# Two cross attentions of a perceiver-style block: one projection run per step in the first, a re-ordered hand-over before the main loop of the second

## The reference

```
# first cross attention (32 heads of 16)
q = layernorm(x) @ Wq.T ;  k_raw = ctx @ Wk.T ;  v_raw = ctx @ Wv.T      # k and v interleaved per head
scores = rmsnorm(q) . rmsnorm(k) * 16**-0.5
x = x + softmax(scores) @ v
...
# second cross attention (16 heads of 32)
qdq(t): s = max(|t|) / 127 over the last axis ;  round(t / s) * s
q = qdq(layernorm(x)) @ qdq(wq).T + bq ;  k, v = split(ctx @ wkv.T + bkv)
o = softmax(q . k / sqrt(32)) @ v
x = x + qdq(o) @ qdq(wp).T + bp
```

## Time and profile before

| | |
|---|---|
| median of three runs | 1500.7 us (1500.62 to 1502.13) |
| the profiled execution's own time | 1501.55 us |
| its span, first to last instruction | 1499.7 us |
| PE busy | 1398.5 us, 93% of the span |
| DVE busy | 1009.4 us, 67% |
| ACT busy | 784.4 us, 52% |
| POOL busy | 82.0 us, 5% |
| first cross attention, main loop | about 36 to 437 us |
| second cross attention, c2 | about 773 to 1012 us |
| c3, c4, c5 | about 1012 to 1020, 1020 to 1174 and 1174 to 1194 us |

### The profile page before, as it was taken

The page is one execution under the profiler, slowest core; times in us unless marked ns, Lnnn a source line. Parts: engine busy times, 40 slices in busy tenths (PEclk is TensorE's granted clock), DMA queues, the critical chain, the costliest instruction groups (busy, mean ns, idle before and its releaser), DMA issues. The chain is left out here.

```text
span 1499.7 us, 31832 instructions
## 1 busy us (share of the span) xinstructions
PE 1398.5 (93%) x11742; PEld 1075.1 (72%) x11742; DVE 1009.4 (67%) x1657; ACT 784.4 (52%) x1134; POOL 82.0 (5%) x73
## 2 busy tenths in 40 slices
PE   6999999999979989999989999978999598899998
PEld 4677776777745468999978787755666365899997
DVE  7666667666654557666647777876999843676664
ACT  3677777777750635554432232227888203555553
POOL 0000000000000400000001111111000000000000
PEclk8999999999999989999999999988999769899999
DMA  5333453333324058565305223218777120676662
GB/s 159 73 84 85 114 115 80 85 86 86 65 64 161 1 203 270 188 213 194 100 29 176 105 107 131 84 57 184 172 172 164 42 55 6 215 255 209 215 219 78
DMA packets 133599, 191.20 MB, mean 127 GB/s; under 512 B 74987, under 2 KB 96717, under 8 KB 130317
## 3 DMA queue, kind: packets, MB, share of 16 engines
q1 hardware_dynamic: 133533, 190.30, 43.7%
HBM read 154.12 MB, written 17.48 MB: 114 GB/s over the span
## 5 line engine op out<-in xcount | busy, mean ns | idle before, releaser
L187 PE MATMUL psum<-m_x_hi,m_gu_hi 128*128 128x256 f32 x780 | 222.2, 285 | 1.8 <-DVE m_h L2406 1.5
L188 PE MATMUL psum<-m_x_hi,m_gu_lo 128*128 128x256 f32 x780 | 221.7, 284 | 0.0
L189 PE MATMUL psum<-m_x_lo,m_gu_hi 128*128 128x256 f32 x780 | 221.6, 284 | 0.0
L1543 DVE TENSOR_REDUCE x_peaks<-psum 128x2048 f32 (+1 forms) x64 | 146.3, 2291 | 50.6 <-PE psum L1421 50.6
L187 PE MATMUL psum<-x_w_hi,x_ctx_hi 128*128 128x256 f32 x512 | 158.6, 310 | 0.0
L187 PEld LDWEIGHTS psum<-m_x_hi,m_gu_hi 128*128 128x128 f32 x780 | 150.1, 192 | 5.4 <-DVE m_h L2406 2.0
L188 PEld LDWEIGHTS psum<-m_x_hi,m_gu_lo 128*128 128x128 f32 x780 | 150.1, 192 | 1.5
L189 PEld LDWEIGHTS psum<-m_x_lo,m_gu_hi 128*128 128x128 f32 x780 | 150.1, 192 | 0.0
L1700 DVE TENSOR_TENSOR e_wqp<-e_wqp,x_probs 128x1024 f32<-128x1024 f32 x124 | 143.1, 1227 | 2.7 <-ACT x_probs L1715 2.5
L188 PE MATMUL psum<-x_w_hi,x_ctx_lo 128*128 128x256 f32 x512 | 144.5, 282 | 0.0
L189 PE MATMUL psum<-x_w_lo,x_ctx_hi 128*128 128x256 f32 x512 | 144.3, 282 | 0.0
(11 more groups left out here) (319 smaller groups left out, 2765.7 us busy)
## 6 DMA issues: line engine op xcount, KB each, us to landing
m_gu_raw<-in_m_gu SPq DMA_DIRECT2D x41, 768.0 KB, 4.2
e_w<-x_keys_dram SPq DMA_DIRECT2D x45, 512.0 KB, 6.8
m_gu_raw<-in_m_gu SPq DMA_DIRECT2D x18, 1024.0 KB, 4.9
x_ctx_raw<-in_ctxT SPq DMA_DIRECT2D x64, 256.0 KB, 2.7
m_dn_raw<-in_m_down SPq DMA_DIRECT2D x16, 768.0 KB, 4.3
m_dn_raw<-in_m_down SPq DMA_DIRECT2D x18, 512.0 KB, 5.1
x_keys_dram<-x_keys_hi SPq DMA_DIRECT2D x16, 512.0 KB, 3.2
x_keys_dram<-e_wqp SPq DMA_DIRECT2D x16, 512.0 KB, 2.7
```

What stands on the lines that cost most here:

```text
L187: pe.matmul(out, a[0], b[0], start=start, stop=False, skip_group_check=True)
L188: pe.matmul(out, a[1], b[0], start=False, stop=False, skip_group_check=True)
L189: return pe.matmul(out, a[0], b[1], start=False, stop=stop, skip_group_check=True)
L1543: dve.tensor_reduce(peaks[:, t, 4 * m:4 * m + 4, bass.ds(k, 1)].rearrange("p h k -> p (h k)"), g.psum[:, at:at + BANKS, :], AX, ALU.max).t ...
```

## The change

Four things are done.

1. In the first cross attention, PE does all of `values` for step n+1 (12 matmuls) in one run behind `keys`, and nothing behind `weigh`. Since the value bank is now full before `weigh` of step n-1 has read the old values, ACT waits for `pv_done` before `take_values`.
2. In c3, PE turns the peaks first and zeroes the banks behind it. The spread of the `wp` scales goes from c3 to c5, where ACT, PE and ACT again do it at the block's start, with waits on `wp_row_taken`. ACT's first Exp with its table load goes from the start of c4 to the end of ACT's list in c3.
3. The loads of `bp` and `bv` go from the start of c4 into c2, behind the twelve DMAs of `q_stack`. The bias add goes from POOL in c4 to DVE in c3. The load of key pair 1 goes from c3 to the start of c4.
4. Names and semaphores follow.

```diff
@@ first cross attention, PE
-                        values((s + 1) % SLOTS, half_of(at + 1), v_part, range(NC // 2))
+                        values((s + 1) % SLOTS, half_of(at + 1), v_part, range(NC))
                     for grp in (2, 3):
                         score(n, s, half, grp)
...
                     for grp in (0, 1):
                         weigh(n, s, grp)
-                    if at + 1 < STEPS:
-                        values((s + 1) % SLOTS, half_of(at + 1), v_part, range(NC // 2, NC))
@@ first cross attention, ACT
                     if at + 1 < STEPS:
+                        act.wait_ge(pv_done, 4 * n + HG)
                         take_values(n + 1, s + 1, v_part)
@@ second, c2, SP (behind the q_stack DMAs)
+                    sp.dma_start(bp[:, :], A["x1_bp"]).then_inc(bp_loaded, 16)
+                    sp.dma_start(bv[:, :], A["x1_bv"]).then_inc(bv_loaded, 16)
@@ second, c3
                     dve.tensor_scalar(peakT[:, :], g.bank[0][0:Y_H, 0:L], -1.0, None, ALU.mult).then_inc(peak_taken, 1)
+                    dve.wait_ge(bp_loaded, 16)
+                    for t in range(NT):
+                        dve.tensor_tensor(g.x[:, t, :], g.x[:, t, :], bp[:, :], ALU.add)
...
-                    for b in g.bank[4:8]:
-                        pe.matmul(b[:, :], g.zeros[:, 0:P], g.zeros[:, :], start=True, stop=False, ...)
                     pe.wait_ge(peak_found, 1)
                     for t in range(NT):
                         last = pe.transpose(g.bank[0][0:Y_H, t * P:(t + 1) * P], peak[:, t, :], g.ident[:, :])
                     last.then_inc(peak_turned, 1)
-                    pe.wait_ge(wp_spread_ready, NC)
-                    for m in range(NC):
-                        last = pe.transpose(g.bank[1][:, m * P:(m + 1) * P], wp_spread[:, m, :], g.ident[:, :])
-                    last.then_inc(wp_row_turned, 1)
+                    for b in g.bank[4:8]:
+                        pe.matmul(b[:, :], g.zeros[:, 0:P], g.zeros[:, :], start=True, stop=False, ...)
...
-                    (four spreads into wp_spread, the wait, the copy to wp_row)
                     act.activation(k_stack[3 * Y_HD:3 * Y_HD + 1, 1, :, :]...)
+                    act.activation(warm[:, :], g.zeros[:, 0:1], ACT.Exp)
...
                     load_keys(sp, 0, 0, slice(NC // 2, NC))
-                    load_keys(sp, 1, 1)
                     sp.wait_ge(peak_placed, 16)
@@ second, c4
-                    pool.wait_ge(bp_loaded, 16)
-                    for t in range(NT):
-                        pool.tensor_tensor(g.x[:, t, :], g.x[:, t, :], bp[:, :], ALU.add)
...
-                    sp.dma_start(bp[:, :], A["x1_bp"]).then_inc(bp_loaded, 16)
-                    sp.dma_start(bv[:, :], A["x1_bv"]).then_inc(bv_loaded, 16)
+                    load_keys(sp, 1, 1)
...
-                    act.activation(warm[:, :], g.zeros[:, 0:1], ACT.Exp)
@@ second, c5: the spread of the wp scales, now into a part of vals and bank 2
+                    for m in range(NC):
+                        act.activation(wp_spread[:, m, :], g.zeros[:, 0:P], ACT.Identity,
+                                       bias=g.x1_grid[:, 1, m:m + 1]).then_inc(wp_spread_ready, 1)
+                    act.wait_ge(wp_row_turned, 1)
+                    act.activation(wp_row[:, :], g.bank[2][:, :], ACT.Copy).then_inc(wp_row_taken, 1)
...
+                    pe.wait_ge(wp_spread_ready, NC)
+                    for m in range(NC):
+                        last = pe.transpose(g.bank[2][:, m * P:(m + 1) * P], wp_spread[:, m, :], g.ident[:, :])
+                    last.then_inc(wp_row_turned, 1)
```

More of the change, by code:

```diff
@@ L1596, in stage_cross1 @@
             peak = sb("peak", [P, NT, Y_H], F32, c3)
+            warm = sb("warm", [P, 1], F32, c3)
             peakT = sb("peakT", [Y_H, L], F32, c3)
[L1598 to L1601, removed]
+            peak_found, peak_turned, peak_taken, peak_placed = (
+                sem(n) for n in ("peak_found", "peak_turned", "peak_taken", "peak_placed"))
             with nc.Block() as block:
@@ L1617, in _ @@
                     last.then_inc(peak_turned, 1)
-                    pe.wait_ge(wp_spread_ready, NC)
-                    for m in range(NC):
-                        last = pe.transpose(g.bank[1][:, m * P:(m + 1) * P], wp_spread[:, m, :], g.ident[:, :])
-                    last.then_inc(wp_row_turned, 1)
+                    for b in g.bank[4:8]:
+                        pe.matmul(b[:, :], g.zeros[:, 0:P], g.zeros[:, :], start=True, stop=False,
+                                  skip_group_check=True)
                 @block.gpsimd
@@ L1628, in _ @@
                 def _(act):
-                    for m in range(NC):
-                        act.activation(wp_spread[:, m, :], g.zeros[:, 0:P], ACT.Identity,
-                                       bias=g.x1_grid[:, 1, m:m + 1]).then_inc(wp_spread_ready, 1)
-                    act.wait_ge(wp_row_turned, 1)
-                    act.activation(wp_row[:, :], g.bank[1][:, :], ACT.Copy)
                     act.activation(k_stack[3 * Y_HD:3 * Y_HD + 1, 1, :, :].rearrange("p h (a n) -> p (h a) n", n=P),
@@ L1650, in stage_cross1 @@
             probs = sb("probs", [P, Y_PAIRS, 2 * L], F32, c4)
-            warm = sb("warm", [P, 1], F32, c4)
             s_ready, probs_ready, pv_done, added = (
@@ L1664, in stage_cross1 @@
             with nc.Block() as block:
-                @block.gpsimd
-                def _(pool):
-                    pool.wait_ge(bp_loaded, 16)
-                    for t in range(NT):
-                        pool.tensor_tensor(g.x[:, t, :], g.x[:, t, :], bp[:, :], ALU.add)
                 @block.sync
                 def _(sp):
-                    sp.dma_start(bp[:, :], A["x1_bp"]).then_inc(bp_loaded, 16)
-                    sp.dma_start(bv[:, :], A["x1_bv"]).then_inc(bv_loaded, 16)
+                    load_keys(sp, 1, 1)
                     with sp.Fori(0, MT // 4 - 1) as i:
@@ L1781, in stage_cross1 @@
         with ExitStack() as c5:
-            oT, inv, o, o16, oqT, y = (vals[:, 2 * i:2 * i + 2, :] for i in range(6))
+            oT, inv, o, o16, oqT, y, wp_spread = (vals[:, 2 * i:2 * i + 2, :] for i in range(7))
+            wp_spread = wp_spread[:, 0, :].rearrange("p (m n) -> p m n", n=P)
             oT, inv = (v.rearrange("p t (b a n) -> p t b a n", b=2, a=2) for v in (oT, inv))
@@ L1786, in stage_cross1 @@
             grid = sb("grid2", [P, NT], F32, c5)
-            turned, inverted, divided, biased, step_done, o_turned, o_taken, projected, scaled = (
-                sem("f_" + n) for n in ("turned", "inverted", "divided", "biased", "step_done", "o_turned", "o_taken",
-                                        "projected", "scaled"))
+            (turned, inverted, divided, biased, step_done, o_turned, o_taken, projected, scaled, wp_spread_ready,
+             wp_row_turned, wp_row_taken) = (
+                 sem("f_" + n) for n in ("turned", "inverted", "divided", "biased", "step_done", "o_turned", "o_taken",
+                                         "projected", "scaled", "wp_spread_ready", "wp_row_turned", "wp_row_taken"))
             def of_tile(b, t):
@@ L1811, in _ @@
                         pe.wait_ge(step_done, GRID_STEPS[-1] * (t + 1))
+                        pe.wait_ge(wp_row_taken, 1)
                         for c in range(NC):
@@ L1837, in _ @@
                                       step_done, GRID_STEPS[-1] * t)
+                    dve.wait_ge(wp_row_taken, 1)
                     for t in range(NT):
```

2 lines of the change are left out of this document (removed).

## The result

The changed kernel takes 1488.9 us (median of six runs, 1483.3 to 1493.3) where the kernel before takes 1501.4 (six runs beside it); the ratio is 0.9911, 95% interval 0.9893 to 0.9928, so 10.8 to 16.1 us less. The forecast was 16.6 less and 1484.1. Two further sets of the same changed code gave medians of 1487.9 and 1489.1.

A forecast was written before the change was run, and what follows sets the result against it. PE's own order was taken to bound the first cross attention, DVE's adds c4; 14.2 plus 2.4 made 16.6 us, so 1500.7 - 16.6 = 1484.1 us, range 1476 to 1491.

The forecast's parts named there:

- one run's fixed cost: First cross attention: a separate projection run on PE costs 0.195 us beyond its matmuls, saved once a step.
- steps 2 to 60: First cross attention: 59 ordinary steps each save 0.195 us by losing one projection run, 11.5 us.
- steps 0, 1, 61, 62: First cross attention: in steps 1, 61 and 62 the moved matmuls fit into waits, 0.9 us each, 2.7 together.
- part 1: First cross attention: one projection run a step in place of two saves 14.2 us.
- start of the chain of adds: c3 to c4: PE's first scores come about 1.1 us sooner, of which 0.4 survives at the second group.
- POOL's interference: Start of c4: POOL's two bias adds stretch DVE's adds; removing them wins 2.0 us.
- rival B: First cross attention: pause behind `weigh` is 0.21 when scores follow, so a step falls by 0.3; 1477.7 us, chance 0.14.
- exp 3: First cross attention: next step's group 1 scores need this exp; PE arrives 0.05 us after its release, so no wait.
- D: First cross attention: exp 3's release reaches PE 0.2 after its end, a step gains only 0.1; 1489.7 us, chance 0.13.
- E: First cross attention: a release costing 0.41 makes each step 0.10 us longer than before; 1501.7 us, chance 0.03.
- Rival C: Start of c4: clock stays at 2.4 GHz over PE's shorter pause, first add some 2 us sooner; 1482.1 us, chance 0.08.
- part 2: Hand-over in c3 and c4: 0.4 from the earlier start and 2.0 from POOL's bias adds save 2.4 us.

The follow-up runs named there:

- repeats: The changed kernel executed again without any change, in two further sets; medians 1487.9 and 1489.1 us.
- late3: The kernel before with nine value matmuls behind `keys` and three behind `weigh`, where it has six and six; 1499.3 us in one execution.
- bias_only: The kernel before with only the bias add moved from POOL in c4 to DVE in c3, its load into c2; 1500.0 us in one execution.
- pool16: The changed kernel with 16 more 128x512 adds on POOL in the middle of c4, their result unused; 1505.6 us in one execution.
- halves: The changed kernel with each key pair in c4 loaded in two halves, each waited for by itself; 1484.9 us in one execution.
- all: The changed kernel with key pairs 0 and 1, ones and first Exp in c2, c4's keys in halves, step 60's keys projected first; 1486.2 us, ratio 0.9905.
- keys_first: The changed kernel with step 60's last keys projected before its first scores; scores of step 59 to those of 63 took 21.67 us, without the edit 22.97.

## Why the prediction was right, and where it fell short

The direction and the range (1476 to 1491) held; the likeliest case's own range, 1482.5 to 1486, did not hold the median. The main mechanism, one run's fixed cost a step, was right. Wrong were the landing of one transfer, two seams of the loop and what was carried through c4: 13.4 measured (1501.4 x 0.0089) for 16.6.

| term | forecast | first profile | repeats |
|---|---|---|---|
| steps 2 to 60 | 11.5 | 10.8 | 10.8 |
| steps 0, 1, 61, 62 | 2.7 | 2.6 | 1.8, 1.9 |
| part 1 | 14.2 | 13.3 | 12.6 |
| start of the chain of adds | 0.4 | 0.05 | 0.4, 0.5 |
| POOL's interference | 2.0 | 1.9 | 1.9, 2.0 |
| given back in c4 | 0 | -1.8 | -0.8, -1.1 |
| sum | 16.6 | 13.5 | 14.1, 14.0 |

- **The run's fixed cost.** Right: 0.187 a step against 0.195, only with the run gone (late3), the pause behind `weigh` 0.42 (rival B fell), exp 3 no wait in an ordinary step (D and E fell: the margin was 0.05 by forecast and 0.11 by the rows above).
- **"The k_stack transpose and the context split get their inputs no later than before."** The transpose got its inputs at the same time, but its output came later. From the start of step 60 its DMA is issued after 7.6 in both kernels; it lands after 10.7 before and after 12.3 now. PE, with steps of 6.0 and 4.6, would be there after 10.6 and waits 1.7, which is nearly what the transfer takes more (4.70 for 3.07). Steps 1, 61 and 62 were priced at a gain of 0.9 each; 62 gained 0.90 and 61 lost 0.82. It is no accident of one profile: the transfer takes 4.70 to 4.81 in all seven profiles with the changed loop, and 3.02 to 3.07 in the five with six or three late matmuls and in the two with the edit of step 60. In the seven a 16 KB load of instructions starts while it is on its way; before, one starts 0.1 us ahead of the landing. Over all fourteen profiles 57 transposing transfers took over 4.2 us, and 49 of them have an instruction load beside them, where the middle one of all those without has 3.1. That the load makes them slow is therefore likely; no run moves it alone.
- **Step 33.** It became longer too, 6.19 to 6.65, since ACT comes out of the change of halves behind. There the forecast had a gain of 0.195 like everywhere.
- **Luck in steps 0 and 1.** The forecast had a gain of 0.9 there; against the profile of before it is 2.5 in the first profile and 1.8 in the repeats, which hides the loss in step 61. Before, the two steps take 17.67 with the granted clock at 0.50 from 48.9 to 52.3. In `bias_only`, with the same code and no such stretch, they take 16.78, and 16.78 - 15.87 of the repeats is the forecast's 0.9. So about 0.9 to 1.6 us of part 1's 12.6 to 13.3 come from where the clock was low in one profile, as far as single profiles can tell.
- **The earlier start.** Right to allow only part of it: the second key half bounds the second group. The peaks landed as the forecast took it, behind the key halves in the queue, at 6.3 for 6.2; PE came 0.7 behind it and not 0.5, so the first scores were 0.8 sooner and not 1.1.
- **POOL.** 2.0 was right, in both directions (bias_only 2.0, pool16 1.08 an add). What failed is that it was carried to the end as if the chain were bound by nothing but itself: "DVE's adds run without a gap". With 2 us less in front, the chain from add 6 to the last takes 133.7 to 134.9 where it took 132.9 to 133.1. Part of it are gaps where a new key pair is needed, and PE's waits for `e_w` were there before as well (6.1 us in eleven). But with all these waits gone (`halves`, `all`) it still takes 133.6. So some 0.5 of what is given back has another cause, which stays open, and how much the key transfers cost isn't told from the spread of c4 among executions.
- **Rival C.** Its condition was not met, so it was not tested: it needs the clock at 2.4 GHz (1.00) when PE's pause before c4 begins, as it was before (1.00 at 1015). In the first profile after, the clock was at 0.50 already from 990.3, ahead of c3, to 1014.2. The pause was 4.3, where the forecast had 3.7 and before it was 4.9. The pause of 3.87 ahead of c3 in the earlier trace rows, which the prediction passes over, says nothing either: the clock was at 0.50 from 1004.7, before it began. Windows of the first profile, in c3, in c4's first and second tile (columns as above):

```profile
1001.00:1002.00 1.00, 0.00 (x0) 0.00 (x0) 0.00 (x0) 0.99 (x2) 0.49 (x1) 0.50 1.05 246
1010.00:1011.00 1.00, 1.00 (x10) 0.43 (x13) 0.32 (x1) 1.00 (x2) 0.00 (x0) 0.50 1.02 201
1016.00:1017.00 1.00, 1.00 (x20) 0.58 (x18) 1.00 (x1) 0.94 (x2) 0.00 (x0) 1.00 0.00 0
```

- **c5 and the loads in c2.** Nothing, as forecast: from DVE's first reciprocal to c5's end both kernels take the same to 0.01 us, and c2 takes 217.4 us from its first reduction for the peaks to c3, before 217.5.
- **What was not priced.** The whole program shifts against the clock's low stretches. In unchanged stages behind c5 that is -6.2 in one profile and +2.3 in the other, as much as part 2's price and its error together.

## What to carry to other kernels

A stall that is taken off the bounding engine is worth at most the distance to the next bound, not its own length: look in the waits of the other engines for one that the late chain covers. Where a loop gets shorter, check its last steps and its seams apart, and compare each transfer's issue and landing there with those of before: a wait of 1.7 us came from one transfer that landed 1.6 later after its issue, not from a later issue. Before a run is taken as proof of a cause, look for the same landmark in a run whose code is the same at that place: `halves` and `keys_first` ended c4 within 0.04 of each other. Judge an edit of one to three microseconds by the distance between landmarks in its own stage, since the same code varied by 10 us as a whole, and know that stage's own spread (1.7 here).

## What the runs showed of the hardware

- In this loop a run of projection matmuls costs about 0.19 us beyond its matmuls, however many they are (3, 6 or 18), and the pause behind matmuls with outputs of 17 rows in four strips is 0.42 whether projection or scores follow; the other changes of kind that show a pause have 0.21.
- VectorE and GpSimd adds with two inputs in SBUF alternate strictly: 2.22 us for one of each (128x1024 on VectorE, 128x512 on GpSimd), where VectorE alone takes 1.14. VectorE's copies of 128x1024 are stretched by GpSimd's adds too, from 0.69 to 1.80 and 1.66.
- A transfer of 16 KB takes 2.2 us alone and 3.4 to 4.8 beside transfers of 256 KB in the same queue; there it lands at the same moment (6.1 to 6.4 us behind c3's start) whether it is issued at 1.5 or at 2.8.
- A transposing transfer of this loop lands 3.0 to 3.3 us after its issue in most cases and 4.2 to 5.0 in 57 of the fourteen profiles' 896, 49 of them with a load of instructions beside it.
